# Two routings that take their weights and most roots from the attention ahead, running sums by TensorE in bf16, and first scores ahead of batch 1's queries

## What is computed

```
x = x + attention0(layernorm(x), ctx)     # 16 heads, causal
x = x + ffn0(layernorm(x))                # 16 experts of width 512, the best 2 of each row
x = x + attention1(layernorm(x), ctx)     # 16 heads, biases, no mask
x = x + ffn1(x)                           # layernorm inside, 7 experts of width 1024 with a capacity, and a shared one
```

```
logits = layernorm(x) @ Wg + bg + bias            # ffn0;  ffn1: (layernorm(x) * ln_g + ln_b) @ Wr
vals, idx = top_k(logits, 2)
w = softmax(vals)                                 # the gates
# ffn1 alone: each (choice, row) gets a running number in its expert's list, first choices ahead of second ones
onehot = one_hot(idx, E_ROUTED)
pos = sum(cumsum(onehot, axis=0) * onehot, -1) - 1
keep = pos < CAPACITY
```

## Time and profile before

| | |
|---|---|
| median of three timed runs | 1297.19 us (1297.01 to 1300.53) |
| the profiled execution's own time | 1293.13 us |
| its span | 1291.5 us |
| PE busy | 1146.9 us (89%) |
| PEld busy | 1015.1 us (79%) |
| DVE busy | 699.7 us (54%) |
| ACT busy | 586.4 us (45%) |
| POOL busy | 352.1 us (27%) |
| mean granted TensorE clock | 0.935 |

### The profile page before, as it was taken

One profiled execution on the slowest core, in us unless ns is written; L12 is line 12 of the kernel. 1 busy time (PEld: TensorE's weight loads), 2 busy tenths in 40 slices (PEclk: granted clock), 3 DMA queues, 4 the chain that ended last, 5 costly groups with the idle time before them and its releaser, 6 DMA issues. The chain is left out here.

```text
span 1291.5 us, 26046 instructions
## 1 busy us (share of the span) xinstructions
PE 1146.9 (89%) x8590; PEld 1015.1 (79%) x8590; DVE 699.7 (54%) x1637; ACT 586.4 (45%) x1191; POOL 352.1 (27%) x469
## 2 busy tenths in 40 slices
PE   5999998759999985888998559999999999999997
PEld 4788886759888873465665559999999999999997
DVE  4755565661222116677777555455555555555556
ACT  3666665202222222676777224344454444444432
POOL 5656540012222205776540025200000000000252
PEclk9899999559999997799999659999999999999999
DMA  7774560537999976567661311122232232322132
GB/s 189 169 168 129 146 175 2 190 139 250 322 334 308 315 242 146 112 131 133 112 112 25 107 58 69 58 78 82 88 109 83 87 106 62 109 83 85 55 95 82
DMA packets 88138, 172.57 MB, mean 134 GB/s; under 512 B 11251, under 2 KB 59949, under 8 KB 81792
## 3 DMA queue, kind: packets, MB, share of 16 engines
q1 hardware_dynamic: 71712, 136.15, 37.9%
q0 software_dynamic: 9584, 29.32, 7.6%
q10 hardware_dynamic: 6768, 6.16, 1.4%
HBM read 133.11 MB, written 39.20 MB: 133 GB/s over the span
## 5 line engine op out<-in xcount | busy, mean ns | idle before, releaser
L2085 PE MATMUL e_ps<-xT_e,wp_e 128*128 128x384 f32 (+1 forms) x1344 | 245.2, 331 | 4.0 <-DVE wp_e L1959 4.0
L2085 PEld LDWEIGHTS e_ps<-xT_e,wp_e 128*128 128x128 f32 x1344 | 221.7, 188 | 5.4 <-issue 4.1
L648 DVE TENSOR_REDUCE att_ps<-att_ps 128x2 f32<-128x512 f32 (+1 forms) x224 | 155.2, 697 | 99.2 <-PE att_ps L989 61.0
L1917 ACT ACTIVATE act_a_e<-e_ps 128x256 f32<-128x256 f32 (+2 forms) x176 | 77.7, 442 | 159.7 <-PE e_ps L2085 158.9
L899 ACT ACTIVATE probs<-att_ps 128x384 f32<-128x384 f32 (+1 forms) x256 | 130.4, 547 | 43.2 <-PE att_ps L1021 29.5
L2015 DVE TENSOR_TENSOR hid_e<-act_a_e,e_ps 128x256 f32<-128x256 f32 (+2 forms) x176 | 87.0, 494 | 116.0 <-ACT act_a_e L1917 106.8
L1921 ACT ACTIVATE hidp_e<-hid_e 128x256 fp32r<-128x256 f32 (+2 forms) x176 | 83.8, 476 | 127.2 <-DVE hid_e L2015 125.4
L2102 PE MATMUL e_ps<-wp_e,hidp_e 128*128 128x256 f32 (+1 forms) x1008 | 138.4, 282 | 2.9 <-DVE xres L1975 1.2
L2017 DVE TENSOR_TENSOR hidp_e<-hid_e,hidp_e 128x256 fp32r<-128x256 f32 (+2 forms) x176 | 87.8, 499 | 95.5 <-ACT hidp_e L1921 95.5
L2102 PEld LDWEIGHTS e_ps<-wp_e,hidp_e 128*128 128x128 f32 (+1 forms) x1008 | 130.7, 183 | 4.9 <-issue 4.1
L1565 ACT ACTIVATE hid_e<-e_ps,b_ahead 128x128 f32<-128x128 f32 x188 | 53.6, 368 | 168.7 <-PE e_ps L1664 168.7
(11 more groups left out here) (225 smaller groups left out, 1912.7 us busy)
## 6 DMA issues: line engine op xcount, KB each, us to landing
w_e<-in_W SPq DMA_DIRECT2D x47, 1024.0 KB, 7.5
w_e<-in_W SPq DMA_DIRECT2D x57, 384.0 KB, 3.0
ks<-parts SPq DMA_DIRECT2D x96, 128.0 KB, 4.5
qs<-parts SPq DMA_DIRECT2D x96, 128.0 KB, 6.0
parts<-cut SPq DMA_DIRECT2D x30, 384.0 KB, 3.0
x_e<-rows SPq DMA_DIRECT2D x8, 768.0 KB, 5.2
done<-y_e ACTq DMA_DIRECT2D x47, 128.0 KB, 5.4
rows<-zeros POOLq DMA_DIRECT2D x8, 736.5 KB, 7.4
```

What stands on the lines that cost most here:

```text
L648: dve.tensor_reduce(tops_at(at[3])[:, qt, x0:x0 + heads], src, AX.X, ALU.max).then_inc(reduced, 1)
L1917: act.activation(act_a[:, u % 2, 0:n], ps[:, AB + u % 2, 0:n], ACT.Silu).then_inc(silu_ready, 1)
L2085: last = pe.matmul(ps[:, bank + u % 2, 0:n], weights(lot, c, pw)[:, (b * DC + d) * P:(b * DC + d + 1) * P], xT[:, px, d, t0:t0 + n], start ...
```

## The change

The routing's weights and row vectors get buffers and a signal outside the blocks and are loaded at the end of SyncE's queue in the attention ahead. GpSimd computes the reciprocal roots of all batches but the last at the end of the attention, by the same Newton steps, once VectorE has copied batch 6's statistics (`measured`). The routing takes ScalarE's root for the last two tiles alone, and asks for it in front of the last batch's norm. The tables `ones`, `before` and `pick` become bf16. VectorE's running sums go; TensorE adds each tile's picks to all later tiles' ranks by `ones` with a broadcast operand. Per quarter a `total` is added up in layer 0; layer 1 makes none. VectorE counts the first choices per partition (`counted`, `firsts`). In layer 1's attention TensorE scores the first two units of batch 0 ahead of batch 1's queries, the wait for the queries being taken moves in front of the second `scoreT`, and ScalarE's root for batch 2 and its table load for the exponential move ahead of its take of batch 1's queries.

```
--- before.py
+++ after.py
-    m["ones"] = sb("ones", [P, P])
-    m["before"] = sb("before", [P, P])
+    m["ones"] = sb("ones", [P, P], BF16)
+    m["before"] = sb("before", [P, P], BF16)
...
+LAST_ROWS = slice((B - 1) * TPB, NT)
...
 # attend_block, SyncE, last
+            for dst, name in zip(router["rows"], router["names"]):
+                sp.dma_start(dst, a[name].partition_broadcast(P)).then_inc(router["loaded"], 16)
+            sp.dma_start(router["wr"][:], a[router["matrix"]].rearrange("(c p) e -> p c e", p=P)).then_inc(router["loaded"], 16)
 # GpSimd, after its last batch
+            pool.wait_ge(measured, 1)
+            known = slice(0, LAST_ROWS.start)
+            newton(pool, m["rstd"][:, known], m["mv"][:, known, 1], spread[:, known], bits[:, known], near[:, known])
 # VectorE, aggregate
-                dve.tensor_copy(m["mv"][:, bass.ds(n * TPB, TPB), :], mv[:])
+                moved = dve.tensor_copy(m["mv"][:, bass.ds(n * TPB, TPB), :], mv[:])
+                if isinstance(n, int) and n == B - 2:
+                    moved.then_inc(measured, 1)
 # ScalarE
+                if f and ye is not None:
+                    square_root(NORM - 1, 1, 3)
+                    act.activation(warm[:], offset[:, 0:1], ACT.Exp)
                 take_whole(f, f, 0)
 # TensorE, batch
+                    if ye is not None and first and g == 0:
+                        pe.wait_ge(taken[0], FEED)
                     scoreT(at, 1)
 # TensorE, batches 0 and 1 ahead
                 turn_rows(f, f)
+                if f and ye is not None:
+                    pe.wait_ge(taken[1], FEED)
+                    for u in range(RING):
+                        score((0, 0, 0, 0), u)
...
-            for w in KINDS:
-                pe.wait_ge(taken[w], FEED)
+            if ye is None:
+                for w in KINDS:
+                    pe.wait_ge(taken[w], FEED)
...
-            for u in range(NU):
+            for u in range(0 if ye is None else RING, NU):
                 score((0, 0, 0, 0), u)
 # route_block, TensorE, rank
-                lo = max(lo, 1)
-                pe.matmul(ranks[:, :, lo:hi], m["ones"][:], upto_tile[:, :, lo - 1:hi - 1], start=False, stop=True, skip_group_check=True)
+                for t in range(lo, min(hi, NT - 1)):
+                    n = NT - 1 - t
+                    pe.matmul(ranks[:, :, t + 1:NT], m["ones"][:], pick[:, :, t].unsqueeze(2).to_broadcast([P, 2, n, E]),
+                              start=False, stop=False, skip_group_check=True)
+
+            def total(q):
+                pe.wait_ge(picked, q + 1)
+                for c in range(2):
+                    last = pe.matmul(ps[:, CB, 0:TQ * E], m["ones"][:], pick[:, c, q * TQ:(q + 1) * TQ].rearrange("p t e -> p (t e)"),
+                                     start=q == 0 and c == 0, stop=q == QUARTERS - 1 and c == 1)
+                return last
 # TensorE, per batch and at the end
                 if n % BQ == BQ - 1 and q:
+                    total(q - 1)
                     rank(q - 1)
...
+            if not capped:
+                total(QUARTERS - 1).then_inc(totals_made, 1)
             rank(QUARTERS - 1)
-            pe.matmul(ranks[:, 1], m["ones"][:], upto_tile[:, 0, NT - 1].unsqueeze(1).to_broadcast([P, NT, E]),
+            pe.wait_ge(firsts_ready, 1)
+            pe.matmul(ranks[:, 1], m["ones"][:], firsts[:].unsqueeze(1).to_broadcast([P, NT, E]),
                       start=False, stop=True, skip_group_check=True).then_inc(ranks_made, 1)
 # VectorE
+                if n == B - 1:
+                    dve.wait_ge(root_ready, 1)
+                    dve.reciprocal(m["rstd"][:, LAST_ROWS], m["rstd"][:, LAST_ROWS])
+                    dve.drain()
...
-                for t in range(q * TQ, (q + 1) * TQ):
-                    if t:
-                        last = dve.tensor_tensor(upto_tile[:, :, t], upto_tile[:, :, t - 1], pick[:, :, t], ALU.add)
...
+            then(dve.tensor_reduce(counted[:], pick[:, 0].rearrange("p t e -> p e t"), AX.X, ALU.add))
+            dve.tensor_copy(firsts[:], counted[:]).then_inc(firsts_ready, 1)
...
-                then(dve.tensor_copy(load[:], ps[:, CB, 0:E]))
+                then(dve.tensor_reduce(load[:], ps[:, CB, 0:TQ * E].rearrange("p (t e) -> p e t", t=TQ), AX.X, ALU.add))
```

More of the change, by code:

```diff
@@ L388, in of, with newton @@
                 return ap[:, lo:lo + n * TPB]
-            y, nh, b, a, off = of(rstd), of(spread), of(bits), of(near), of(offset)
             at = stats_at(f, (f % 2,) if ye is not None and f >= NORM else None, 0)
-            mean, var = of(mean_var[:, :, 0], at), of(mean_var[:, :, 1], at)
+            y, off, a = of(rstd), of(offset), of(near)
+            newton(eng, y, of(mean_var[:, :, 1], at), of(spread), of(bits), a)
+            eng.tensor_tensor(a, of(mean_var[:, :, 0], at), y, ALU.mult)
+            eng.drain()
+            return eng.tensor_scalar(off, a, -1.0, None, ALU.mult)
+        def newton(eng, y, var, nh, b, a):
             eng.tensor_scalar(nh, var, LN_EPS, None, ALU.add)
@@ L408, in root @@
             eng.drain()
-            eng.tensor_tensor(a, mean, y, ALU.mult)
-            eng.drain()
-            return eng.tensor_scalar(off, a, -1.0, None, ALU.mult)
         @block.sync
@@ L1173, in _, with route_block @@
                 project(B - 1, t)
-def route_block(nc, m, layer, E, a, hall, shared=None, biases=None, rows=None, W=None, ctxT=None, ahead=None):
+def route_block(nc, m, layer, E, a, hall, router, shared=None, biases=None, rows=None, W=None, ctxT=None, ahead=None):
     ctx = ExitStack()
@@ L1212, in route_block @@
         keymax = sb("keymax", [P, NT])
-        pick = sb("pick", [P, 2, NT, E])
-        upto_tile = sb("upto_tile", [P, 2, NT, E])
+        pick = sb("pick", [P, 2, NT, E], BF16)
+        counted = sb("counted", [P, E])
+        firsts = sb("firsts", [P, E], BF16)
         work = sb("work", [P, N2, E])
@@ L1232, in route_block @@
         BQ, TQ = B // QUARTERS, NT // QUARTERS
[L1234 removed]
+        const_ready = sem("const_ready")
         var_ready, root_ready = sem("var_ready"), sem("root_ready")
@@ L1341, in _ @@
                 if n % BQ == BQ - 1 and q:
+                    total(q - 1)
                     rank(q - 1)
-            pe.wait_ge(picked, QUARTERS)
-            for c in range(2):
-                last = pe.matmul(ps[:, CB, 0:E], m["ones"][:], upto_tile[:, c, NT - 1], start=c == 0, stop=c == 1)
-            last.then_inc(totals_made, 1)
+            if not capped:
+                total(QUARTERS - 1).then_inc(totals_made, 1)
             rank(QUARTERS - 1)
-            pe.matmul(ranks[:, 1], m["ones"][:], upto_tile[:, 0, NT - 1].unsqueeze(1).to_broadcast([P, NT, E]),
+            pe.wait_ge(firsts_ready, 1)
+            pe.matmul(ranks[:, 1], m["ones"][:], firsts[:].unsqueeze(1).to_broadcast([P, NT, E]),
                       start=False, stop=True, skip_group_check=True).then_inc(ranks_made, 1)
@@ L1399, in pick_two @@
                     then(dve.tensor_reduce(keymax[:, tiles], key[:, tiles], AX.X, ALU.max))
-                    then(dve.tensor_tensor(pick[:, c, tiles], over_tiles(fall[:]), over_experts(keymax[:, tiles]), ALU.is_equal))
-                    if c == 0:
+                    chosen = dve.tensor_tensor(pick[:, c, tiles], over_tiles(fall[:]), over_experts(keymax[:, tiles]), ALU.is_equal)
+                    if c:
+                        chosen.then_inc(picked, 1)
+                    else:
+                        dve.drain()
                         then(dve.scalar_tensor_tensor(out=left[:, tiles], in0=pick[:, 0, tiles], scalar=MASKED, in1=logits[:, tiles],
@@ L2134, in two_layers, with router_of @@
         parts = [nc.dram_tensor(f"parts_{layer}", (2, B, PARTS, DC, P, S), BF16, kind="Internal").ap() for layer in range(2)]
+        def router_of(layer, E, matrix, names, width):
+            wr = ctx.enter_context(nc.sbuf_tensor(f"wr_{layer}", [P, DC, E], F32))
+            table = ctx.enter_context(nc.sbuf_tensor(f"router_table_{layer}", [P, 2, width], F32))
+            signal = ctx.enter_context(signals(nc, m["resting"]))
+            return {"wr": wr, "table": table, "rows": [table[:, x, :] for x in range(2)], "matrix": matrix, "names": names,
+                    "loaded": signal(f"router_loaded_{layer}")}
+        routers = [router_of(0, E0, "Wg", ("bg", "bias"), E0), router_of(1, E1, "Wr", ("ln_g", "ln_b"), D)]
         with nc.sbuf_tensor("vals_0", [P, NT, H, DK], F32) as vals:
-            attend_block(nc, m, 0, W[0], parts[0], vals, (xe1,), a["ctxT"], x=a["x"], masks=a["masks"], constants=True)
+            attend_block(nc, m, a, 0, W[0], parts[0], vals, (xe1,), a["ctxT"], x=a["x"], masks=a["masks"], constants=True, router=routers[0])
         with ExitStack() as layer, signals(nc, m["resting"]) as signal:
```

44 lines of the change are left out of this document (13 added, 31 removed).

## The result

The changed kernel takes 1284.12 us (median of four, 1282.63 to 1285.74) against 1297.54 us for the kernel before beside it: ratio 0.9885, 95% interval 0.9859 to 0.9911. Forecast were 1288.0 us and a gain of 9.2; at that ratio the 1297.19 us from which the forecast started become 1282.3, under the 1283 where its range began. The direction was right, the size was not: even the upper end of the interval, 0.9911, is a gain of 11.5 us. Two later sets gave 0.990 (0.9873 to 0.9927) and 0.9885 (0.9849 to 0.992).

A forecast was written before the change was run, and what follows sets the result against it. Stages with barriers bound the kernel; in the routings a late start, TensorE at half clock, then VectorE's chain. Routing 1 8.4, routing 0 1.0, attention 1 0, end -0.2: 9.2 us, from 1297.19 to 1288.0, range 1283 to 1293.5.

The forecast's parts named there:

- Routing 1: Layer 1's routing: 8.4 us gained, 3.6 at its start and 4.8 behind the last pick.
- the start: Routing 1's first norm waits for GpSimd's `upto` and no longer for loads: 3.6 us sooner.
- what follows the last pick: Routing 1: ranks read 2.4 us behind the picks, today 7.23; gain 4.8 us, bounds 3.9 and 5.0.
- Routing 0: Layer 0's routing: start 1.0 us sooner, last logits 0.55 later, no wait for totals; gain 1.0, bounds -1.5 and 2.5.
- Rival C: Routings: only the starts count, TensorE's accumulations in one bank run no faster than f32 ones; 1293.2 us, chance 0.09.
- GpSimd's roots: End of both attentions: about 6.2 us of small operations, with two to three us of cover before attention's last operation.
- Rival E: GpSimd's roots end over 2 us behind the attention and delay `const_ready`; five us late in each: 1298, chance 0.03.
- VectorE's last operations: End of attention: GpSimd's roots could block them through the shared port; 0.8 us, in the range, not the sum.
- Attention 1: First scoreT 1.3 us sooner, given back at the wait for batch 2's query stack: zero; bounds 3 gained, 2 lost.
- Rival A: Attention 1 passes its gain of 1.3 to 3 us, the first group waiting less: about 1286, chance 0.09.
- Rival B: TensorE's clock rises in routing 0 behind the first rank, 3 to 4 us: about 1284, chance 0.04.
- The end of the kernel: Two more sets of semaphores to clear: 0 to 0.5 us lost, taken at 0.2.

The follow-up runs named there:

- loads_alone: Kernel before with only the routings' weight and vector loads moved to the end of SyncE's queue in the attention ahead, all roots by ScalarE; ratio 0.9956.
- sums_alone: Kernel before with only the bf16 tables, TensorE's running sums, the totals per quarter and the count of firsts; ratio 0.9908, in a second set 0.9946.
- ranks_deferred: Changed kernel with routing 0's totals and ranks of the first three quarters made behind the last logits; ratio to the kernel before 0.9876.
- att_alone: Kernel before with only the new order at the start of attention 1, TensorE's and ScalarE's parts; ratio 0.997.
- dense_more: Changed kernel with 8 bf16 matmuls of 512 columns added on TensorE behind routing 0's first rank; ratio to the kernel before 0.9921.
- dense_before: Kernel before with 8 bf16 matmuls of 512 columns added on TensorE behind routing 0's first rank; ratio 1.0003.
- both_warm: Kernel of both with 20 bf16 matmuls of 512 columns added on TensorE ahead of batch 1's turn in attention 1; ratio to the kernel before 0.9866.
- both: Changed kernel with the edits of tables_late and ranks_deferred together; ratio to the kernel before 0.9837.
- both_again: The kernel of both, unchanged, run a second time; ratio to the kernel before 0.9836.
- tables_late: Changed kernel with VectorE's wait for GpSimd's tables moved from the first norm to the first pick; ratio to the kernel before 0.9854.

## Why the prediction was 4 us short: right in both routings, wrong in attention 1

**Routing 1, right.** 8.4 us predicted, 8.7 measured (44.8 in the mean of five profiles, 36.1 after). In the pair of profiles, 8.6 in all, the start gave 3.6 of 3.6 and what follows the last pick 5.0 of 4.8. The ranks are read 2.2 us after the last pick instead of 2.4, since the narrow matmuls took no longer than about their columns: 1.48 us between the first `ones` matmul and that of the firsts, where 1.87 was taken. That left VectorE's own 2.2, which the prediction had beside it.

**Routing 0, right without the rise.** 1.0 us predicted, 1.35 measured in the pair. The last logits came 0.12 us later where 0.55 was forecast. Rival C fell with both: its fifteen accumulations in one bank would have taken 6 us and took 1.48.

**GpSimd's roots, right and without use in this kernel.** They end at 225.36 in attention 0, with the last statistics copy at 228.41 + 0.17, inside the cover. Rival E did not come, and loads_alone shows that nothing would be lost without them. Nor did they hold up VectorE's last operations, for which 0.8 us was kept in the range: between attention 0's last two statistics copies lie 9.8 us in the mean of the twelve profiles with the roots and 10.0 in the eight without.

**Attention 1, the step that failed.** "I take zero" rested on one row, the wait of 1.92 us at 568.31, taken for a fixed barrier. The first half of the step was right: the first scoreT was to come 1.3 us sooner and comes 2 us sooner. But among the ten profiles with the old order, only two (before and sums_alone) have that wait; in the others the stack was there in time, and a sooner start could pass. With the new order seven of ten have a wait of 0.2 to 2.9 us there, and still the first batch is 1.9 us shorter in the mean. So the wait takes back a part and not the whole: 1.3 us (error 0.9) are left at the end of the stage, and the timed runs give 2.4 (1.4) to 4.4 (0.8). The bound of 3 was there, and all but the last of these lie inside it; the value taken should not have been zero. Rival A had the mechanism.

**Rival B, undersized.** It had a chance of 0.04 because TensorE was busy at half clock for all of the earlier trace rows. The sum held nothing for it. The profiles show it in three of nine executions, at 3.4 to 3.6 us, in the place the prediction named: about 1.2 us in the mean. The Trainium skill, page "TensorE: Matmul & The Clock Gate", section "What's actually happening", says that sustained activity releases the throttle. The rows agree with it in five of eleven profiles with bf16 matmuls there, and go against it for these routings' float32 stream, busy without a gap at 0.50, and for the 3.1 us of bf16 in ranks_deferred.

**The end of the kernel, a little undersized.** 0.2 us was taken, with a bound of 0.5. The time outside the span is 1.7 us in the runs of the kernel before and 2.15 in those of every kernel with the whole change in its routings: 0.45. With loads_alone, sums_alone and att_alone it stays at 1.7, so none of these parts alone brings it, and what does is open.

**The balance.** Routings without the rise 10.0 us, the rise 1.2, attention 1 1.3, the end -0.45: 12.0 of the 13.4 measured, for which 9.2 was forecast. The 1.4 that are left are about the error of the means (1.1 for the changed kernel's runs, 0.9 for attention 1). What stays open: att_alone and sums_alone gave more time in the runs than their profiles show in the changed stages (3.9 to 4.4 against 1.3 to 1.9, and 7 to 12 against 4.5 to 8.6), and the parts one by one add up to more than the whole.

## What to carry to other kernels

A wait seen in one execution is no barrier: before a gain is set to zero because a later wait absorbs it, the same point is to be found in a second profile. Nor is a gain at the first batch the gain of the stage: later waits can still take a part of it, so the whole stage is to be compared over several profiles. When a load is moved off the start of a stage, look at once at what is late next and whether its reader needs it yet; here moving that wait to its true reader was worth 4.5 us. Work that no one waits for until the end doesn't belong into the stream of the engine that sets the pace.

## What the runs showed of the hardware that was not expected

TensorE's clock stayed at 0.50 in the kernel before's routing 0 while float32 matmuls kept TensorE busy for 16 us on end (234 to 250), and it rose in the same routing behind 1.7 us of bf16 matmuls in three of nine executions, and in both in which eight of 512 columns stood there (2.56 us in dense_more, behind the 1.7; 3.29 in dense_before, alone). Behind 3.1 us of bf16 matmuls it stayed at 0.50 in ranks_deferred and both_warm and rose in both and both_again. Bf16 matmuls of 210 down to 14 columns, each with a load of 128 weights, followed each other at 0.1 us in the mean at half clock, 1680 columns in 1.48 us. GpSimd's `upto` of routing 1 (128x49) took 0.35 us in the changed kernel, beside an idle VectorE, and 0.75 us in tables_late, both, both_again and both_warm, beside a busy one.
